# Self attention of a two layer decoder: five instead of three of a weight quantiser's sixteen trials on VectorE

## What is computed

```python
k = einsum('ihd,bpd->biph', W_K, x); q = ...; v = ...
scores = einsum('biph,biqh->biqp', k, q)
attn = softmax((scores * mask - 1e10 * (1 - mask)) / sqrt(d_head))
z = einsum('biqp,biph->biqh', attn, v)
out = einsum('df,bqf->bqd', W_O, z_flat)
```

```python
base = max(amax, 1e-8) / QMAX
for s in SHRINKS:                      # 16 values from 0.4 to 1.0
    scale = base * s
    deq = clip(round(wb / scale), -QMAX, QMAX) * scale
    err = sum((deq - wb) ** 2)
    best_err, best_scale = where(err < best_err, (err, scale), (best_err, best_scale))
```

## Time and profile before

| | us |
|---|---|
| three runs: median (lowest to highest) | 3277.67 (3277.07 to 3279.28) |
| the profiled execution | 3273.77 |
| its span, first to last instruction | 3272.0 |
| the self attention's slots in it (first to last L2846) | 1830 to 2647 |

### The profile page before, as it was taken

The page is one execution under the profiler, slowest core; times in us unless marked ns, Lnnn a source line. Parts: engine busy times, 40 slices in busy tenths (PEclk is TensorE's granted clock), DMA queues, the critical chain, the costliest instruction groups (busy, mean ns, idle before and its releaser), DMA issues. The chain is left out here.

```text
span 3272.0 us, 49538 instructions
## 1 busy us (share of the span) xinstructions
PE 2815.0 (86%) x16144; PEld 2521.0 (77%) x16144; DVE 2121.1 (65%) x4210; ACT 1679.4 (51%) x4263; POOL 1660.9 (51%) x2073
## 2 busy tenths in 40 slices
PE   5699999775999999985898899999999955659998
PEld 4578888664788888874898788888888844548998
DVE  3468887644777888886355477767776766764333
ACT  1056666502888887863554456566555523324222
POOL 0067777501776766663344478888887860000000
PEclk9899999876999999998899899999999976779999
DMA  3545555424333333332412312212121113323101
GB/s 126 182 134 156 159 152 152 138 87 149 119 112 111 111 98 109 99 116 61 121 47 66 118 52 96 69 44 89 44 78 41 48 59 107 109 80 107 41 26 31
DMA packets 218751, 314.50 MB, mean 96 GB/s; under 512 B 49042, under 2 KB 114678, under 8 KB 216406
## 3 DMA queue, kind: packets, MB, share of 16 engines
q1 hardware_dynamic: 218518, 311.58, 30.4%
HBM read 215.15 MB, written 96.37 MB: 95 GB/s over the span
## 5 line engine op out<-in xcount | busy, mean ns | idle before, releaser
L925 POOL TENSOR_TENSOR mh_quant_d<-mh_quant_a,mh_quant_d 128x512 f32<-128x512 f32 x208 | 277.2, 1333 | 17.4
L1000 ACT ACTIVATE mh_quant_d<-mh_quant_d 128x512 f32<-128x512 f32 x256 | 159.8, 624 | 119.6 <-POOL mh_quant_d L925 119.6
L903 DVE TENSOR_REDUCE mh_quant_err<-mh_quant_d 128x8 f32<-128x512 f32 x256 | 173.5, 678 | 38.2 <-ACT mh_quant_d L1000 36.3
L919 POOL TENSOR_SCALAR mh_quant_d<-mh_quant_a 128x512 f32<-128x512 f32 x208 | 132.7, 638 | 127.6 <-DVE mh_quant_err L903 80.0
L1645 PE MATMUL bank<-ga_eT,ga_v 128*128 128x400 f32 (+1 forms) x384 | 168.4, 520 | 29.8 <-DVE ga_zl L1831 29.6
L1602 PE MATMUL bank<-ga_xt,ga_wqh 128*128 128x400 f32 x512 | 177.4, 409 | 1.6 <-DVE ga_xt L164 1.6
L1795 ACT ACTIVATE ga_e<-ga_e,ga_nm 100x361 f32<-100x361 f32 x256 | 152.7, 597 | 39.1 <-DVE ga_nm L1890 37.8
L958 POOL TENSOR_TENSOR ga_quant_d<-ga_quant_a,ga_quant_near 128x512 f32<-128x512 f32 x128 | 165.3, 1291 | 14.0 <-DVE ga_quant_err L903 3.5
L1371 POOL TENSOR_TENSOR kv_krs<-kv_kms,minus_half 128x4 f32<-128x4 f32 x48 | 50.0, 1043 | 229.3 <-DVE kv_kms L1359 227.9
L2342 POOL TENSOR_TENSOR fq_var<-fq_mv,eps_ln 100x1 f32<-100x1 f32 x16 | 3.7, 230 | 319.4 <-DVE fq_mv L2285 319.4
L1791 ACT ACTIVATE ga_e<-ga_e,ga_rs 100x361 f32<-100x361 f32 x256 | 152.6, 596 | 18.6 <-DVE ga_rs L1872 18.6
(11 more groups left out here) (435 smaller groups left out, 10614.7 us busy)
## 6 DMA issues: line engine op xcount, KB each, us to landing
keys_turned<-kv_kt SPq DMA_DIRECT2D x16, 1448.0 KB
ga_kt<-keys_turned SPq DMA_DIRECT2D x64, 362.0 KB, 2.9
ga_xt<-x_turned SPq DMA_DIRECT2D x48, 400.0 KB, 5.1
mh_xt<-x_turned SPq DMA_DIRECT2D x48, 400.0 KB, 4.8
qkv<-m_rows SPq DMA_DIRECT2D x16, 1000.0 KB
kv_rows<-qkv SPq DMA_DIRECT2D x50, 320.0 KB, 3.4
raw<-x SPq DMA_DIRECT2D x64, 200.0 KB
kv_ctx<-in_ctx SPq DMA_DIRECT2D x32, 256.0 KB
```

Source lines behind the costliest of these rows:

```text
L903: nc.vector.tensor_reduce(self.of(self.err, i)[:, s, :], self.error(i, s), AX, ALU.add).then_inc(self.summed.sem, 1)
L925: nc.gpsimd.tensor_tensor(e, a[:], e, ALU.subtract).then_inc(self.diff.sem, 1)
L1000: nc.scalar.activation(self.error(i, s), self.error(i, s), ACT.Square).then_inc(self.squared.sem, 1)
```

## The change

The quantiser of the self attention stage gets its own list of VectorE trials: 2, 5, 8, 11 and 14 instead of 3, 8 and 13. The other quantisers, in the stages before, keep the old list.

```diff
 QUANT_ON_DVE = (3, 8, 13)
+MHA_ON_DVE = (2, 5, 8, 11, 14)
...
-        qz = Quantiser(ph, ctx, t["L1_ffn_w_proj"], w_proj_q, 0, NC, on_pool=True, depth=2, on_dve=QUANT_ON_DVE)
+        qz = Quantiser(ph, ctx, t["L1_ffn_w_proj"], w_proj_q, 0, NC, on_pool=True, depth=2, on_dve=MHA_ON_DVE)
```

## The result

| | before | after |
|---|---|---|
| median of the comparison, us | 3277.37 (3272.37 to 3279.28, 4 runs) | 3302.44 (3301.33 to 3303.39, 4 runs) |
| ratio to before, 95% interval | | 1.0083 (1.0071 to 1.0095) |
| span of the profiled execution, us | 3272.0 | 3299.9 |
| the 64 slots, first to last score, us | 814.8 | 847.9 |
| last score to the next stage's first matmul, us | 66.6 | 63.6 |

The change makes the kernel 25 us slower, not 8. The direction and the place are as forecast; the size is three times that. All of it lies in the slots (+33.1 us). The stage's end gives 3.0 us back, and the stage begins 2 us earlier.

A forecast was written before the change was run, and what follows sets the result against it. TensorE was taken as the bound, with no slack behind VectorE's additions in position 2. Terms 14.5 - 2.6 - 4 = +7.9 us on the profiled 3273.8 gave 3281.7, or 3285.6 against the runs' median 3277.7; range 3273 to 3302.

The forecast's parts named there:

- What bounds the kernel: Self attention stage: TensorE is the bound; VectorE's work added in position 1 is paid at full price in `mh_acc` waits.
- (a): Position 1, one VectorE trial more: 0.97 us a group, paid 15 times, +14.5 us; bounds 4.5 and 28.5.
- trial 5 finds GpSimd idle: Position 1: GpSimd's trial 4 is over and 6 not yet released, so VectorE's added trial costs 1.07 us.
- (b): Position 0, one VectorE trial more: price nothing; without cover up to 1.1 us in each of 12 groups.
- (c): Less waiting for GpSimd: ScalarE's squares -1.6 us, position 0 waits in slots 28 and 44 -1.0; together -2.6, bounds 0 and -5.
- (d): Stage's end, where GpSimd's trials set the end: one trial fewer there gives -4 us, bounds -1 and -7.
- (e): TensorE's clock: half clock after some waits loses 1.6 us a stretch; nothing taken, up to +6 for the upper end.
- slow trials and clock: Rival, clearly slower: added trial meets GpSimd, longer position 2 waits cost half-clock stretches; +18 to +30, about 3301 us; chance 0.20.
- Contention undone: Rival, faster: GpSimd out of VectorE's way in position 1, -0.4 us a group, -12.6 in all, 3265 us; chance 0.13.

The follow-up runs named there:

- before_narrow: Kernel before, with three of the four GpSimd instructions of this stage's trials cut to one column of each block of 64: 3241.81 us, 0.9902.
- v_four: Kernel before with trials 0, 8, 11, 14 on VectorE instead of 3, 8, 13, none in position 1: 3273.88 us, 0.9996.
- e_pos1: Kernel before with trials 2, 5, 8, 13 on VectorE, so only position 1 gets a trial more: 3300.71 us, 1.0077.
- v_none1: Kernel before with trials 8, 11, 14 on VectorE, as many as before but none in position 1: 3273.25 us, 0.9999.

## Why the prediction was wrong, step by step

- **What bounds the kernel: right.** The growth is in the waits for `mh_acc`, in positions 1 and 2. VectorE's 22.3 us in position 1 came back as 22.2 of waiting, at full price, and group by group within 0.4 us but for the last two, where the waits of slots 57, 58, 61 and 62 grew by 1.1 us a group more than VectorE's list.
- **(a), position 1: direction right, size wrong, +14.5 foretold and +22.2 measured.** The trial's own part was nearly exact: 1.07 less 0.27 over 15 groups is 12.0, measured 12.6. The contention was counted as +0.17 a group, 2.6 in all, and was 9.7. Two of its rows came out reversed: L982 was to lose 0.5 and lost nothing (0.26 us in slot 33, where GpSimd's trial began 0.16 us after it; over the position it gained 4.5), while L992 and L994, which the sum didn't hold, lost 10.7. And "trial 5 finds GpSimd idle" was true only in slots with weight pieces, where other VectorE work gives GpSimd time to end trial 4. The step that failed is the one where slot 33 stood for 15 groups: the six groups like it grew by 0.87 us of waiting each, slots 22, 38 and 54 by 2.0. The upper bound of 28.5 did hold the value. The lower one of 4.5 was worked out wrongly: by its own terms (L982 not held up, the next L2847 at 0.17 instead of 0.74) it is -0.1 us for a group and not 0.3.
- **(b), position 0: right.** Its waits for pieces stayed at 2.55 us, and the kernel with this part alone is not slower but 0.3% faster.
- **(c), less waiting for GpSimd: half there.** ScalarE's waits for GpSimd fell from 109 us to 56.5 in 32 waits. Slots 28 and 44, with the waits of 2.87 and 3.2 us, came down to 2.55 as foretold, and with them position 0 by 1.4 us. The other 1.6 us, foretold for groups like that of slot 25, brought nothing: the waits for `mh_acc` in position 1 did fall, from 6.9 to 1.4 us, but came back in position 2 of the same groups (slot 25 had 1.16 us and slot 26 none before, afterwards it is none and 3.24), since VectorE's list is the bound through both.
- **(d), the stage's end: right**, -3.0 for a foretold -4.
- **(e), the clock: the largest miss, and the step that failed most.** Nothing was taken in the sum and 6 allowed; the rest of positions 1 and 2 cost 11.8 net, 16.0 of it in position 2. The trace of before had the warning: 0.50 behind a wait of position 0, 0.52 behind the wait of 1.89 us for `mh_acc` in slot 61, and full clock behind the 1.54 us of slot 58 (1.67 in slot 62). What was missing is the second step: once (a) lengthens waits past what the trace shows without loss, they bring stretches at 1.2 GHz. Here all nine waits for `mh_acc` of 2.1 us and more in position 2 did, and the six of 1.5 us did not.

The forecast for the slots was 14.5 - 2.6 = +11.9 and they grew by 33.1. The 21.2 between divide into waits 7.7, position 2's clock 16.0, position 1's rest -4.2, and 1.7 of small differences. Of the rivals, "slow trials and clock" (3301, given a chance of 0.20) came true, by nearly its mechanism: L910 does meet GpSimd, though not in the slots with pieces, and the clock costs more than its 6. "Contention undone" had the same rows and the wrong sign: fewer trials on GpSimd didn't mean fewer beside VectorE's long instructions. The Trainium skill (SBUF — State Buffer, "Who interferes with whom") says that a `tensor_scalar` of VectorE in a two-port mode and an operation of GpSimd block each other, and that a reduction never contends with GpSimd. The rows agree as far as they go (whether L910 and L992 run in such a mode they don't say): all 252 of L904 in the kernel after last 0.65 to 0.69 us, where L992 goes from 0.72 to 1.38 and L910 from 0.43 to 1.40. The amount over a position hangs on the order of the two lists.

What stays open: whether before_narrow's 22 us of slots are all contention or in part GpSimd's own length, and why a wait of one and the same length is followed by half clock in one slot and not in another (below).

## What to carry to other kernels

When work moves between two engines that hold each other up, count what runs at the same time afterwards, slot by slot and for each kind of slot, not the number of operations left on the other engine: five trials cost 25 us in one list and 10 in another. Where a change lengthens a matmul engine's waits, put a price on the clock behind each wait that gets longer than those that the trace shows at full clock. And where a wait can't be shortened, matmuls that nobody reads ahead of it can be worth the issue: here 14 to 17 us in one kernel and 10 to 13 in another.

## What the hardware showed that was not expected

- In the runs without added matmuls no position-2 slot whose wait was at most 1.5 us took over 0.6 us more, beside its wait, than the shortest of that slot in any run. All nine waits of 2.1 to 4.8 us for `mh_acc` in the changed kernel cost 1.6 to 2.5 us more behind them than the slots took before. But length alone doesn't decide: waits of 3.0 us in slots 58, 62 of v_four and 42 of e_pos1, of 2.5 in slots 26 and 42 of v_none1 and of 2.1 in slot 54 of e_pos1 cost at most 0.3 us (the granted clock behind each of them was 1.00), and the 2.55 us in position 0 cost 0, 1.3 to 1.6 or 2.7 to 2.8 us, in the same slot of one kernel and the next.
- VectorE's L910 (128x512, f32 to 8-bit integers) took 0.43 us with GpSimd idle and 1.40 beside L926. GpSimd's L926 in turn took 1.60 beside L910 and 1.81 beside L992, and 1.3 in most of its rows (139 of 176). Both sides pay.
- Taking work off the engine that is late can gain nothing: v_none1, with no trial in position 1, was no faster than before, because GpSimd's row of eight then set the pace there.
